# A loaded in two halves, pairs 2 to 6 of W transposed later, pair 2 loaded ahead of the stores of A0, B0 and A0 transposed in the same two banks

## The chip, the cores and the metric

The kernel runs on one core of a Trainium2 chip. The metric is the device time of one execution in microseconds, lower is better. A core has five engines that run their own instruction streams and meet at semaphores: TensorE (PE in the profile; its weight loads are listed as PEld), VectorE (DVE), ScalarE (ACT), GpSimd (POOL) and SyncE (SP). Here nearly all DMA transfers are issued by SP, so SP's stream is the order in which data are asked for.

## The reference

The input `x` has 8 batch entries of 512 tokens and 2048 columns. Two layers are added to it, one after the other:

```python
# layer 0: a low-rank adapter of the batch entry, rank 16
Bx = einsum('bni,bri->bnr', x, B0[adapter_ids])
x = x + einsum('bnr,bor->bno', Bx, A0[adapter_ids])
# layer 1: a dense product, and a gated mixture of 8 adapters of rank 16
base = einsum('btd,od->bto', x, W)                       # W is 2048 x 2048
logits = einsum('btd,ed->bte', x, Wr) + 5 * one_hot(language_ids)
gates = softmax over the two largest logits, zero elsewhere
lora = einsum('bter,bte,eor->bto', einsum('btd,erd->bter', x, A), gates, Bm)
x = x + base + 2 * lora
```

## The kernel before

**Arithmetic.** All large products are float32 made of two parts: an operand is split into a rounded high part and the rest (`wh` and `wl`, `xh0` and `xl0`), and three products (high by high, low by high, high by low) are summed in PSUM. ScalarE makes the high parts, VectorE the low ones. From batch entry 1 on, the dense product goes by a scheme with seven products of halves. It needs sums and differences of blocks of the transposed W; these are computed once, during batch entry 0, and stored to the DRAM tensor `t_scr`.

**The start** (`pe_start`, `act_start`, `dve_start`, `sp_start`). TensorE warms up with 18 transposes of the identity (`warm`), transposes A (`a_transpose`, four groups of 4 blocks), the small weights (`small_transpose`) and batch entry 0 of x (`x_transpose`, 16 units u). For each unit `aux_products` multiplies x by A, Wr and B0 of its entry. Between these steps s = 0 to 15 stand the transposes of all B0 rows (`b0_transpose`, 4 groups) and of all A0 rows (`a0_transpose`, 8 groups). `a0_rows_hi` and `a0_rows_lo` make the two parts of A0; when they are done (semaphore `c_ar` at 2), SP copies 16 rows of them to `a0g` (`G_ROWS`), which TensorE needs for `delta`, and stores all of them to `a_scr` for later entries. `g_products` prepare how layer 1's small products see layer 0. `delta` and `adapt` add layer 0 to x, two units of 128 columns at a time, and `first_hi` and `first_lo` split the result.

**Batch entry 0** (`pe_main`, `act_main`, `dve_main`, `sp_main`). There are 36 slots i, four groups of nine. A slot of the first eight of a group multiplies x by one pair of blocks of W: a first half (`first_products(e, i, 0)`) and a second half of 12 matmuls each. The ninth is the gated adapter product. W comes in as it lies in memory and is transposed here: pair g is loaded by `first_load(g)` into one of two buffers of `raw` (four DMAs of 128 KB), transposed in two halves by `w_transpose(g, h)`, which go through PSUM bank 7 one after the other, and kept by ScalarE (`w_keep(g, h)`) in one of two other buffers of `raw`. From there ScalarE and VectorE split it (`pair_hi`, `pair_lo`), VectorE computes four sums (`w_sums`) into the single buffer `tst`, and SP stores the blocks (`w_store`) and the sums (`w_sums_store`) to `t_scr`.

**What is ordered by what.** Every engine goes through its list in order, and the lists are written out by hand. `first_load(g)` waits until pair g - 2 is transposed; `w_transpose` of a half waits until the half before it is kept; `w_keep(g, 0)` waits for the sums of pair g - 2 and for the landing of the store of pair g - 2 (`d_bs`); `w_sums(g)` waits for the landing of the store of the sums before it (`d_ts`), since there is one `tst`. In SP's list `first_load(i + 5)` stands behind `w_sums_store(i + 2)`. In slot 3 VectorE also makes a difference for the adapter weights (`bt_difference`), whose inputs `bt` come from a load of Bm (`bn`), eight copies on GpSimd and four transposes on TensorE (`bt_transpose`, slots 1 and 2); `bt_store` and `bt_difference_store` write them, and `first_load(8)` reads them back.

In the texts "slot 3" is the part of TensorE's list for i = 3, and (7, 0) is `w_transpose(7, 0)`. A slot without waits lasts about 7 us: two halves of 12 matmuls and some four short transposes or deltas.

## Time and profile before

| | us |
|---|---|
| median of 3 runs | 1611.52 (1611.37 to 1612.34) |
| the profiled execution, whole time | 1611.55 |
| its span, first to last instruction | 1609.8 |
| TensorE busy in it | 1580.3 |
| VectorE busy in it | 1180.3 |
| ScalarE busy in it | 754.5 |

The profiled execution is 0.03 us from the median of the runs. 1.75 us lie outside the span. Times of rows are counted from the start of the span. A row of the timeline gives the start, the duration, the engine, the line of the kernel and the instruction; in brackets stands how long the engine had been idle before it and what released it. Of SP, whose rows say SPq, the duration is that of issuing, not that of the transfer.

### The profile page before, as it was taken

What the parts mean: (1) busy time and instruction counts of PE and PEld (TensorE: products, weight loads), DVE (VectorE), ACT (ScalarE), POOL (GpSimd) and SP (SyncE); (2) the same over time, 40 slices, a digit from 0 to 9 for tenths busy, and PEclk for the clock granted to TensorE, in tenths of its full rate; (3) what the DMA queues carried; (4) which work ended last, traced back from release to release, by engine and by line L of the source; (5) the groups of instructions that cost most, each with busy time, mean ns of one, the idle gap of its engine ahead of it and who ended that gap; (6) DMA issues with size and microseconds to landing.
All of it is one profiled execution on the core that took longest, in us unless ns stands there. A gap on an engine that the chain in (4) does not pass through costs nothing.

```text
span 1609.8 us, 21189 instructions
## 1 busy us (share of the span) xinstructions
PE 1580.3 (98%) x7762; PEld 1334.6 (83%) x7762; DVE 1180.3 (73%) x1603; ACT 754.5 (47%) x988; POOL 9.3 (1%) x19
## 2 busy tenths in 40 slices
PE   8799999999999999999999999999999999999998
PEld 8677887788888888888888888888888888888887
DVE  5664443687678876987778976888769877787665
ACT  6544443254444544454544544445444544445443
POOL 1100000000000000000000000000000000000000
PEclk9899999999999999999999999999999999999999
DMA  9888796879787887779876897879977787576664
GB/s 266 230 232 250 200 251 190 212 213 229 201 224 227 222 212 205 234 212 238 207 217 219 215 233 186 239 230 222 217 197 236 221 226 202 198 231 204 207 222 158
DMA packets 397018, 351.45 MB, mean 218 GB/s; under 512 B 250538, under 2 KB 323546, under 8 KB 395866
## 3 DMA queue, kind: packets, MB, share of 16 engines
q1 hardware_dynamic: 396642, 349.56, 78.7%
q8 instruction: 62, 1.02, 0.3%
q10 hardware_dynamic: 272, 0.52, 0.1%
q14 instruction: 42, 0.34, 0.1%
HBM read 280.75 MB, written 68.82 MB: 217 GB/s over the span
## 4 chain that ended last, share of the span: by engine, by line
PE 92%; issue 3%; DMA 2%; SPq 1%; DVE 1%; POOL 0%; ACT 0%; POOLq 0%; ACTq 0%; DVEq 0%
PE pb L779 27%; PE pb L780 27%; PE pb L781 27%; PE pb L388 4%; PE pb L390 3%; PE pb L542 2%; PE pb L682 1%; DMA t_scr<-tst 1%; DMA a0n<-in_L_cond_A_dram 1%; PE pb L321 0%; DMA bt_scr<-bt 0%; SPq L658 0%; DMA raw<-in_L_cond_W_dram 0%; PE pb L957 0%; POOL xst L1262 0%
## 5 line engine op out<-in xcount | busy, mean ns | idle before, releaser
L775 DVE TENSOR_TENSOR wl<-raw,wh 128x1024 fp32r<-128x1024 f32 (+1 forms) x456 | 554.8, 1217 | 333.9 <-ACT wh L771 333.6
L771 ACT CAST wh<-raw 128x1024 fp32r<-128x1024 f32 (+1 forms) x456 | 477.1, 1046 | 681.6 <-PE pb L781 674.5
L779 PE MATMUL pb<-wh,sh 128*128 128x512 f32 x1568 | 612.9, 391 | 0.5 <-DVE ost L815 0.5
L780 PE MATMUL pb<-wl,sh 128*128 128x512 f32 x1568 | 611.6, 390 | 0.0
L781 PE MATMUL pb<-wh,sl 128*128 128x512 f32 x1568 | 611.2, 390 | 0.0
L781 PEld LDWEIGHTS pb<-wh,sl 128*128 128x128 f32 x1568 | 294.3, 188 | 62.8
L779 PEld LDWEIGHTS pb<-wh,sh 128*128 128x128 f32 x1568 | 294.6, 188 | 56.1 <-DVE wl L775 0.9
L780 PEld LDWEIGHTS pb<-wl,sh 128*128 128x128 f32 x1568 | 294.6, 188 | 55.0
L388 PE MATMUL pb<-awb,xah 128*128 128x304 f32 x512 | 138.7, 304 | 0.0
L390 PE MATMUL pb<-awb,xal 128*128 128x256 f32 x512 | 134.5, 280 | 0.0
L779 PE MATMUL pb<-wh,xh 128*128 128x512 f32 x256 | 105.2, 411 | 0.9 <-DVE ost L815 0.8
L781 PE MATMUL pb<-wh,xl 128*128 128x512 f32 x256 | 101.2, 395 | 0.0
L780 PE MATMUL pb<-wl,xh 128*128 128x512 f32 x256 | 101.1, 395 | 0.0
L388 PEld LDWEIGHTS pb<-awb,xah 128*128 128x128 f32 x512 | 96.4, 188 | 4.4
L390 PEld LDWEIGHTS pb<-awb,xal 128*128 128x128 f32 x512 | 96.5, 188 | 4.2
L621 DVE TENSOR_TENSOR sl<-pool_a,sh 128x512 fp32r<-128x512 f32 x120 | 82.0, 684 | 0.0
L693 ACT COPY raw<-pb 128x512 f32<-128x512 f32 x64 | 37.7, 589 | 77.8 <-PE pb L682 69.1
L616 ACT CAST sh<-pool_a 128x512 fp32r<-128x512 f32 x120 | 73.5, 613 | 0.0
L363 DVE TENSOR_TENSOR xal<-pool_a,xah 128x512 fp32r<-128x512 f32 x88 | 61.3, 696 | 6.0 <-ACT xah L358 5.7
L549 DVE TENSOR_TENSOR pool_a<-pool_a,pb 128x512 f32<-128x512 f32 x88 | 58.6, 679 | 9.1 <-PE pb L542 9.1
L358 ACT CAST xah<-pool_a 128x512 fp32r<-128x512 f32 x88 | 54.8, 623 | 14.5 <-DVE pool_a L267 13.9
L781 PEld LDWEIGHTS pb<-wh,xl 128*128 128x128 f32 x256 | 48.5, 189 | 10.7
(139 smaller groups left out, 1271.3 us busy)
## 6 DMA issues: line engine op xcount, KB each, us to landing
raw<-t_scr SPq DMA_DIRECT2D x392, 512.0 KB, 4.3
xst<-in_x_dram SPq DMA_DIRECT2D x768, 32.0 KB, 3.9
raw<-in_L_cond_W_dram SPq DMA_DIRECT2D x128, 128.0 KB, 3.9
t_scr<-tst SPq DMA_DIRECT2D x32, 512.0 KB, 4.8
raw<-bt_scr SPq DMA_DIRECT2D x28, 512.0 KB, 3.8
out_dram<-ost SPq DMA_DIRECT2D x28, 512.0 KB, 4.5
out_dram<-u SPq DMA_DIRECT2D x28, 512.0 KB, 3.4
t_scr<-raw SPq DMA_DIRECT2D x32, 256.0 KB, 4.0
```

What stands on the lines that cost most here:

```text
L358: e.copy(x_high(n, u).rearrange("p k t -> p (k t)"), two(n, q, kp)).then_inc(c_xh, 1)
L363: e.tensor_tensor(out=x_low(n, u).rearrange("p k t -> p (k t)"), in0=two(n, q, kp), in1=x_high(n, u).rearrange("p k t -> p (k t)").bitcast ...
L388: e.matmul(pb[:, aux_bank(n, u // 8) + t, 0:2 * AW], x_high(n, u)[:, k, toks], cols[:, 0:2 * AW], start=u % 8 == 0 and k == 0, stop=False)
L390: last = e.matmul(pb[:, aux_bank(n, u // 8) + t, 0:LOW], x_low(n, u)[:, k, toks], cols[:, 0:LOW], start=False, stop=u % 8 == 7 and k == 1)
L549: e.tensor_tensor(out=two(n, q, kp), in0=two(n, q, kp), in1=pb[:, delta_bank(n, u), :], op=ALU.add)\
L616: e.copy(sh[:, h % SR, :, :].rearrange("p k t -> p (k t)"), two(b, SUM_QUARTER[product], kp)).then_inc(c_sph, 1)
L621: e.tensor_tensor(out=sl[:, h % SR, :, :].rearrange("p k t -> p (k t)"), in0=two(b, SUM_QUARTER[product], kp), in1=sh[:, h % SR, :, :].rea ...
L771: e.copy(pair_split(wh, g), pair_source(g)).then_inc(c_wh, 1)
L775: e.tensor_tensor(out=pair_split(wl, g), in0=pair_source(g), in1=pair_split(wh, g).bitcast(f32), op=ALU.subtract).then_inc(c_wl, 1)
L779: e.matmul(o, h, wh[:, g % RING, k, :], start=start, stop=False)
L780: e.matmul(o, h, wl[:, g % RING, k, :], start=False, stop=False)
L781: return e.matmul(o, l, wh[:, g % RING, k, :], start=False, stop=stop)
```

## The change

- **A.** The one load of A (1024 KB) is two loads of half its columns, each with a semaphore of its own; the second stands behind the load of x block 1. Groups 2 and 3 of its transposes, and their splits, move from ahead of the first `aux_products` to steps 0 and 1. Four more warm-up transposes stand behind the transposes of x units 0 and 1.
- **B0 and A0.** The transposes of B0 move from steps 3 to 6 to steps 5 to 8, those of A0 rows (first four groups) from 7 to 10 to steps 8 to 11; both now use banks 2 and 3. The second accumulator of `aux_products` moves to banks 0 and 1. `a0_rows_hi` and `a0_rows_lo` move from steps 11 and 12 to 12 and 13. SP issues the load of x block 4 among the loads of B0.
- **End of the start.** (2, 0) leaves it, (1, 1) goes behind the deltas 2 and 3, and the groups of `g_products` around `bx_transpose` and the deltas 0 and 1 are cut one tile earlier. VectorE makes `w_sums(0)` before `pair_lo(0)`.
- **SP.** `first_load(2)` and the load of Bm go ahead of the stores to `a_scr`, which are taken apart.
- **Slots 0 to 3.** The table `W_AT` gives the W transposes of each slot: ahead of the first half, between the halves, behind the second. `pair_hi`, `pair_lo`, `w_sums`, `w_sums_store` of pairs 2 to 5 move by one slot (`next_pair`), and those of pair 5 stand with those of pair 4 in slot 3. The loads of pairs 4 to 8 move one slot later in SP's list. From slot 4 on all is as before.

```diff
@@ pe_main, act_main, dve_main, sp_main @@
+        W_AT = {0: ((), ((2, 0),), ((2, 1),)), 1: (((3, 0),), ((3, 1),), ()),
+                2: (((4, 0),), ((4, 1),), ((5, 0),)), 3: (((5, 1),), ((6, 0),), ((6, 1),))}
+        for i in range(4, SLOTS0):
+            more = i + 3 < SLOTS0 and (i + 3) % 9 != 8
+            W_AT[i] = (((i + 3, 0),), ((i + 3, 1),), ()) if more else ((), (), ())
+        def next_pair(i):
+            return i + 1 if i < 4 else i + 2
...
@@ pe_start @@
-            warm(e)
+            warm(e, 18)
             for u in range(2):
                 x_transpose(e, 0, u)
+            warm(e, 4)
...
-            g_products(e, range(12, 16))
-            w_transpose(e, 1, 1)
+            g_products(e, range(11, 16))
             for u in range(2, 4):
                 delta(e, 0, u)
-            w_transpose(e, 2, 0)
+            w_transpose(e, 1, 1)
@@ dve_main @@
-                pair_lo(e, i + 2)
+                if i:
+                    pair_lo(e, next_pair(i))
...
-                if i + 2 < SLOTS0 and (i + 2) % 9 != 8:
-                    w_sums(e, i + 2)
+                if i and next_pair(i) < SLOTS0 and next_pair(i) % 9 != 8:
+                    w_sums(e, next_pair(i))
                 if i == 3:
+                    pair_lo(e, 5)
+                    w_sums(e, 5)
                     bt_difference(e)
@@ sp_main @@
-                if i + 2 < SLOTS0 and (i + 2) % 9 != 8:
-                    w_sums_store(e, i + 2)
+                if i and next_pair(i) < SLOTS0 and next_pair(i) % 9 != 8:
+                    w_sums_store(e, next_pair(i))
+                if i < 5:
+                    first_load(e, i + 4)
+                if 4 <= i < SLOTS0 - 5:
+                    first_load(e, i + 5)
                 if i == 3:
+                    w_store(e, 5)
+                    w_sums_store(e, 5)
                     bt_store(e)
                     bt_difference_store(e)
-                if i + 5 < SLOTS0:
-                    first_load(e, i + 5)
```

The change moves instructions, and three places show it. The first is SP behind the last row parts of A0 (`c_ar`). Before, the 16 rows for `a0g` are followed by the two stores to `a_scr`, then come the loads of pair 2 (`raw<-in_L_cond_W_dram`):

```order
L1293 DMA a0g<-a0n 16x2048 [waits c_pool,c_ar]
L1293 DMA a0g<-a0n 16x2048
L1293 DMA a0g<-a0p 16x2048
L1295 DMA a_scr<-a0n 128x2048
L1295 DMA a_scr<-a0p 128x2048
L658 DMA raw<-in_L_cond_W_dram 128x2x128 [waits c_wt]
L658 DMA raw<-in_L_cond_W_dram 128x2x128 x3
```

Now pair 2 comes first, then the stores of pair 0, the load of Bm (`ost<-in_L_cond_B_dram`) and one of the two stores; the next load is that of pair 3:

```order
L1308 DMA a0g<-a0p 16x2048
L657 DMA raw<-in_L_cond_W_dram 128x2x128 [waits c_wt]
L657 DMA raw<-in_L_cond_W_dram 128x2x128 x3
L715 DMA t_scr<-raw 128x2x256 [waits c_wc]
L716 DMA t_scr<-raw 128x256
L721 DMA t_scr<-tst 128x4x256 [waits c_t]
L1312 DMA ost<-in_L_cond_B_dram 128x8x256
L1313 DMA a_scr<-a0n 128x2048
L657 DMA raw<-in_L_cond_W_dram 128x2x128 [waits c_wt]
```

What moved: 1 MB of stores each way around the loads of pairs 2 and 3, and the load of Bm, which before stood behind the loads of pair 3.

The second place is the end of TensorE's start. Before, from the last `g_products` to the first matmul of slot 0:

```order
L1066 MATMUL pb<-awb,a0l 128x304
L682 MATMUL pb<-ident,raw 128x128 [waits c_wc]
L682 MATMUL pb<-ident,raw 128x128 x3
L542 MATMUL pb<-bxt,a0g 128x256 [waits c_x1]
L542 MATMUL pb<-bxt,a0g 128x256
L542 MATMUL pb<-bxt,a0g 128x256 [waits c_x1]
L542 MATMUL pb<-bxt,a0g 128x256
L682 MATMUL pb<-ident,raw 128x128 [waits c_wc,d_raw0]
L682 MATMUL pb<-ident,raw 128x128 x3
L682 MATMUL pb<-ident,raw 128x128 [waits c_wc]
L682 MATMUL pb<-ident,raw 128x128 x3
L779 MATMUL pb<-wh,xh 128x512 [waits c_l0,c_wl]
```

Now:

```order
L1077 MATMUL pb<-awb,a0l 128x304
L541 MATMUL pb<-bxt,a0g 128x256 [waits c_x1]
L541 MATMUL pb<-bxt,a0g 128x256
L541 MATMUL pb<-bxt,a0g 128x256 [waits c_x1]
L541 MATMUL pb<-bxt,a0g 128x256
L681 MATMUL pb<-ident,raw 128x128 [waits c_wc]
L681 MATMUL pb<-ident,raw 128x128 x3
L778 MATMUL pb<-wh,xh 128x512 [waits c_l0,c_wl]
```

What moved: the two transposes of pair 2, of which the first waits for its load (`d_raw0`), are no longer ahead of slot 0's products.

The third place is VectorE in slot 3. Before, behind the two `adapt` (`pool_a<-pool_a,pb`) and the two `first_lo` (`xl<-pool_a,xh`) of deltas 10 and 11, come the four sums of pair 5 and the difference `late<-bt`:

```order
L549 TENSOR_TENSOR pool_a<-pool_a,pb 128x512 [waits c_dl] x2
L569 TENSOR_TENSOR xl<-pool_a,xh 128x2x256 [waits c_h0] x2
L702 TENSOR_TENSOR tst<-raw 128x256 [waits d_ts,c_wc]
L703 TENSOR_TENSOR tst<-raw 128x256
L705 TENSOR_TENSOR tst<-tst,raw 128x256 [waits c_t]
L707 TENSOR_TENSOR tst<-raw,tst 128x256 [waits c_t]
L1106 TENSOR_TENSOR late<-bt 128x1024 [waits d_ag,d_gs,c_btc]
```

Now the sums of pair 4, then pair 5's low part, its sums and the difference:

```order
L701 TENSOR_TENSOR tst<-raw 128x256 [waits d_ts,c_wc]
L702 TENSOR_TENSOR tst<-raw 128x256
L704 TENSOR_TENSOR tst<-tst,raw 128x256 [waits c_t]
L706 TENSOR_TENSOR tst<-raw,tst 128x256 [waits c_t]
L774 TENSOR_TENSOR wl<-raw,wh 128x1024 [waits c_wh]
L701 TENSOR_TENSOR tst<-raw 128x256 [waits d_ts,c_wc]
L702 TENSOR_TENSOR tst<-raw 128x256
L704 TENSOR_TENSOR tst<-tst,raw 128x256 [waits c_t]
L706 TENSOR_TENSOR tst<-raw,tst 128x256 [waits c_t]
L1117 TENSOR_TENSOR late<-bt 128x1024 [waits d_ag,d_gs,c_btc]
```

What moved: the sums of pair 4 came into this slot beside those of pair 5, and a wait for the store of the one (`d_ts`) stands ahead of the other.

## Rows read from the trace of the kernel before

**Rows 1.** The page, part 1: busy time, share, instructions.

```profile
PE 1580.3 (98%) x7762; PEld 1334.6 (83%) x7762; DVE 1180.3 (73%) x1603; ACT 754.5 (47%) x988; POOL 9.3 (1%) x19
```

**Rows 2.** Windows: stretch, its length, busy by engine, granted clock, DMA share, GB/s.

```profile
10.00:11.00 1.00, 0.83 (x9) 0.59 (x7) 0.43 (x1) 1.00 (x2) 0.00 (x0) 0.74 1.03 385
...
54.00:55.00 1.00, 0.00 (x0) 0.00 (x0) 0.91 (x3) 0.85 (x2) 0.00 (x0) 0.93 0.90 246
...
65.00:66.00 1.00, 1.00 (x6) 0.75 (x4) 0.00 (x0) 0.00 (x0) 0.00 (x0) 0.95 1.15 348
...
400.00:800.00 400.00, 400.00 (x1926) 337.41 (x1925) 316.81 (x402) 192.28 (x243) 0.00 (x0) 1.00 0.82 219
```

**Rows 3.** Timeline of TensorE in the start: start, duration, instruction, idle before.

```profile
5.51 1.81 PE L321 MATMUL pb<-ident,xst 128*128 128x128 f32 x8
9.25 1.10 PE L963 MATMUL pb<-ident,an 128*128 128x128 f32 x8 [1.94 <-DMA an<-in_L_cond_A_dram]
...
16.68 0.60 PE L388 MATMUL pb<-awb,xah 128*128 128x304 f32 x1
...
50.21 0.63 PE L542 MATMUL pb<-bxt,a0g 128*128 128x256 f32 x4
```

**Rows 4.** Timeline of TensorE around slots 0 and 1.

```profile
57.22 1.11 PE L682 MATMUL pb<-ident,raw 128*128 128x128 f32 x4 [4.34 <-DMA raw<-in_L_cond_W_dram]
60.70 1.12 PE L682 MATMUL pb<-ident,raw 128*128 128x128 f32 x4 [2.36 <-ACT raw L693]
61.47 0.78 PE L779 MATMUL pb<-wh,xh 128*128 128x512 f32 x1
...
71.56 0.65 PE L1094 MATMUL pb<-ident,xst 128*128 128x128 f32 x4 [1.74 <-POOL xst L1262]
```

**Rows 5.** Timeline of TensorE: (6, 0), (7, 0) and (9, 0).

```profile
88.11 0.60 PE L682 MATMUL pb<-ident,raw 128*128 128x128 f32 x4
...
95.39 0.62 PE L682 MATMUL pb<-ident,raw 128*128 128x128 f32 x4
...
111.18 0.66 PE L682 MATMUL pb<-ident,raw 128*128 128x128 f32 x4 [2.26 <-DMA raw<-in_L_cond_W_dram]
```

**Rows 6.** Timeline of SP's queue: start, time of issuing, transfer, count.

```profile
3.94 1.40 SPq L283 DMA_DIRECT2D ost<-in_x_dram  x2
...
43.17 1.25 SPq L1293 DMA_DIRECT2D a0g<-a0n  x2
...
47.71 5.99 SPq L658 DMA_DIRECT2D raw<-in_L_cond_W_dram  x4
...
59.41 0.49 SPq L1301 DMA_DIRECT2D ost<-in_L_cond_B_dram  x1
...
89.43 2.64 SPq L658 DMA_DIRECT2D raw<-in_L_cond_W_dram  x4
...
95.92 0.36 SPq L722 DMA_DIRECT2D t_scr<-tst  x1
...
104.29 2.82 SPq L658 DMA_DIRECT2D raw<-in_L_cond_W_dram  x4
```

**Rows 7.** DMA issues from 0 to 140 us: count, KB each, median us to landing.

```profile
ost<-in_x_dram SPq DMA_DIRECT2D x4, 512.0 KB, 9.1
...
ost<-in_L_cond_B_dram SPq DMA_DIRECT2D x1, 1024.0 KB, 8.0
...
a0g<-a0p SPq DMA_DIRECT2D x1, 128.0 KB, 5.1
```

**Rows 8.** Line 722 (five stores of the sums), 60 to 100 us.

```profile
DMA to landing us min/median/max: 3.8/4.6/6.3
```

**Rows 9.** Timeline of VectorE: sums of pair 5, then sums of pair 6.

```profile
94.33 0.42 DVE L702 TENSOR_TENSOR tst<-raw 128x256 f32<-128x256 f32 x1
...
102.12 0.42 DVE L702 TENSOR_TENSOR tst<-raw 128x256 f32<-128x256 f32 x1
```

**Rows 10.** Timeline of GpSimd: the eight copies of Bm.

```profile
67.41 4.10 POOL L1262 COPY xst<-ost 128x256 f32<-128x256 f32 x8 [37.10 <-DMA ost<-in_L_cond_B_dram]
```

More of the change, by code:

```diff
@@ L1165, in act_start @@
             small_hi(e)
-            for m in range(2, 4):
-                a_hi(e, m)
             x_keep_act(e, 2)
@@ L1208, in dve_start @@
             small_lo(e)
-            for m in range(2, 4):
-                a_lo(e, m)
             x_keep_dve(e, 3)
@@ L1409, in act_main @@
                         sum_hi(e, 1, 0, kp)
-                if i and more:
-                    w_keep(e, i + 3, 1)
+                for n in (1, 2):
+                    for g, h in W_AT[i][n]:
+                        w_keep(e, g, h)
                 if i in (17, 25):
```

132 lines of the change are left out of this document (67 added, 65 removed).

## The prediction

> **What bounds the kernel now.** I read the page first, then TensorE's timeline with its idle times, then SP's and VectorE's lists at the places where TensorE waits. TensorE is busy for 1580.3 us of the span of 1609.8 us [rows 1], and from 400 to 800 us it is never idle [rows 2]; nothing that the change touches lies there. So the change can only move how early TensorE gets through the start and slots 0 to 8, and every microsecond by which it is early at their end is a microsecond of the total. The reader is to look for three things. In the start, TensorE waits 1.94 us for A and its clock then falls: at 10 to 11 us the granted clock is 0.74 on the mean [rows 3, 2], the fall from the level of 2.4 GHz to that of 1.2 GHz. Ahead of slot 0 it waits 4.34 us for pair 2 and 2.36 us for pair 2's first half to be kept [rows 4], and the clock falls again from about 54.9 us (0.93 in the row of 54 to 55) to 65.05 us (0.95 in the row of 65 to 66) [rows 2]. Then come 1.74 us for GpSimd's copies of Bm [rows 4] and 2.26 us for pair 9 [rows 5]. The sum is worked against the profiled execution (1611.55 us with 1.75 us outside the span), which stands 0.03 us from the median, so I take the two as equal.
>
> **The start, to the first aux product.** The half of A asked for first has 512 KB less ahead of it than A as a whole, which held TensorE until 9.25 us; the x transposes end at 7.32 us [rows 3]. I take it as landed by then: the wait of 1.94 us goes, the four added warm-up transposes (about 0.55 us, half of the 1.10 us of eight [rows 3]) lie in what was idle. What comes next late is x block 2, needed two transposes later: it is the first of two loads at 3.94 us and takes about 9 us [rows 6, 7], so 12.9 us, as many bytes being ahead of it as before. The first aux product then starts at about 13.4 us instead of 16.68 us [rows 3], 3.3 us earlier. The two groups of A that move behind it cost their 0.9 us there, so 2.4 us are left; the idle time ahead of x block 2 may let the clock fall once more, which would cost up to 1.7 us (half of 3.4 us, a third of the spell from 54.9 to 65.05 us [rows 2]; bounds of this term 0.7 and 3.4 us). B0's transposes wait less for their loads, A0's stand behind GpSimd's reordering as before; x block 6 is needed about 1 us early, which I count inside the bounds. Take 2.2 us.
>
> **Rows of A0 and the first deltas.** `c_ar` came at 43.17 us [rows 6]. The row splits are one step (1.9 us) later in the lists, which takes back most of the 2.2: SP starts on the `a0g` rows at about 43.3 us. Its last piece is issued about 1.3 us after and takes 5.1 us [rows 6, 7], so 49.6 us at most, 48.6 us with a DMA queue that has no stores of `a_scr` behind. TensorE would be ready for delta 0 at 47.7 us (50.21 less 2.2 less one tile), so here a new wait of 1 to 2 us stands; delta 0 runs at 49.3 us against 50.21 us [rows 3].
>
> **Slot 0.** Behind delta 0 VectorE needs 3.2 us for two `adapt` and two `first_lo`, so slot 0's first product runs at 52.5 us (52.0 to 53.5). Before it ran at 61.47 us [rows 4]: 9.0 us earlier, the waits of 4.34 and 2.36 us and two transposes at the low clock. Pair 2, loaded right behind the rows of `a0g`, is issued from 45.2 us instead of 47.71 us, without the 2 MB of stores ahead that stretched its issue to 5.99 us [rows 6]; it lands at about 51 us and (2, 0) in the middle of slot 0, at 55.7 us, doesn't wait. Its cover is 4.7 us. Slot 0 now has the work that slot 3 had: two halves, two deltas and two W transposes. From (6, 0) to (7, 0) these took 7.28 us with 0.4 us of another product among them [rows 5], so 6.9 us: to 59.4 us.
>
> **Slot 1.** The load of Bm took 8.0 us from 59.41 us [rows 6, 7]; now it is issued at about 49.5 us, lands at 57.3 us, and GpSimd's eight copies take 4.1 us more [rows 10], so 61.2 us against 71.56 us before [rows 4]. TensorE waits 1.7 us, as before. With 7.8 us of work (slot 3's and two more transposes of 0.44 us) slot 2 begins at 69.0 us. Pair 3 has until 61.7 us, and lands by about 60, as 3.9 MB are asked for from 45 us on at some 0.3 MB per us.
>
> **Slot 2.** Pair 4's load has moved behind the second store of `a_scr` and the late rows of `a0g` in SP's list. By the issue times of before for these it is asked for at about 64.6 us, and takes 5.9 us (pair 7's took from 89.43 us to (7, 0) at 95.39 us at most [rows 5, 6]): 70.5 us, a new wait of about 1.1 us at (4, 0). Deltas 8 and 9 end at 74.7 us, VectorE's sums of pair 3 behind them at 78.8 us, and (5, 0) can be kept only then, so slot 3, which now starts with (5, 1), starts at 79.5 us. Before, slot 3 started at 88.11 us [rows 5]. The lead is at its largest about here: 8.6 us, bounds 6.5 and 10.5 us.
>
> **Slot 3 to (9, 0): where the lead goes.** This is the largest term. I count from the start of slot 3. VectorE finishes the sums that stand behind deltas 10 and 11 at +7.8 us. Before these were pair 5's (begun at 94.33 us, stored at 95.92 us, with slot 3's start at 88.11 us [rows 9, 6, 5]), now pair 4's. Three things hang on it. SP stores the sums, and only then loads pair 7: asked for at +8.2, landed at +14.1 us. TensorE has done slot 3 at +9.2 us (it waits some 1.8 us for pair 6, too, whose load has slid in the same way), so (7, 0) waits about 4.4 us; before, (7, 0) ran at +7.3 us with no wait [rows 5]. Second, VectorE must see pair 4's sums landed before pair 5's: 4.6 us (3.8 to 6.3) [rows 8], so pair 5's sums end at +14.0 us. Third, behind them in VectorE's list are the difference (1.2), pair 6's low part (1.2), the gate's first steps (2.1), `adapt` and `first_lo` of delta 12 (2.0), and then pair 6's sums (1.6): +22.0 us. Before, pair 6's sums began at 102.12 us, +14.0 us [rows 9, 5], and ended at +15.6 us. Behind these sums SP stores them, reads `bt` back (0.8) and asks for pair 9, at +23.2 us; from there it took 6.9 us before (104.29 us to 111.18 us [rows 5, 6]), and 5.9 us with an emptier queue. So (9, 0) runs at +29.6 us, with bounds +28.0 and +31.3 us; TensorE's own work with the wait for pair 7 would have it there at +27.8 us. Before it was +23.1 us. The change gives back 6.5 us of 8.6 us: 2.1 us are left.
>
> **Behind (9, 0)** the lists are the old ones and their waits depend on the same chain of sums, so they shift with it. The long wait for pair 7 lets the clock fall, as the wait of 4.34 us did [rows 2, 4]; most of that is hidden, since TensorE is 1.8 us ahead of pair 9. I charge 0.5 us. Sum: 1611.5 - 2.1 + 0.5 = 1609.9 us.
>
> **A rule of the skill.** The landing rows bear the largest term: 512 KB of sums took 3.8 to 6.3 us [rows 8]. The Trainium skill, DMA: Bandwidth & Descriptors, section "Anatomy of one DMA", gives a fixed 2.0 us and bytes over 436 GB/s for a transfer, an estimate of 3.2 us for 512 KB; it was fitted on GpSimd's path, and the rows here lie 0.6 us and more above it. By it the chain of slot 3 would be some 3 us shorter, which is the first rival taken a little further.
>
> **The rivals.** *First, transfers land at their shortest.* In the changed kernel TensorE waits more in slots 2 to 4, and the queue is emptier. With 3.8 us instead of 4.6 us for the store and 5.2 us for pairs 7 and 9 the chain ends at +28.0 us, and at slot 3 Bm and pair 4 would bring another 1 us: 1611.5 - (9.6 - 4.9) = 1606.8 us. For it speaks the DMA share below 0.82 in mid kernel [rows 2]; against it the 0.90 to 1.15 of the rows up to 66 us [rows 2].
>
> *Second, the lead is kept.* If the sums of pair 4 were not what pair 7's load waits for, say because SP and VectorE run well ahead, 8 us would stay: 1603.5 us. Against it stands the order of both lists; only a mistake of mine in reading them makes this one true.
>
> *Third, slower: the clock.* The wait at (7, 0) and the one at (9, 0) each put the clock to the low level. The spell of before lasted 10.2 us [rows 2], and the products ran at half speed from 61.47 us [rows 4] to its end. If the low level lasts 7 us in slot 4 it costs 3.5 us, of which 1.8 us are hidden, and again 3.5 us behind (9, 0) with nothing to hide it: 1609.4 + 1.7 + 3.5 = 1614.6 us. It decides from the point at which TensorE's waits at (7, 0) and (9, 0) are as long as the 1.94 us that preceded the fall at 10.5 us; against it, 2.26 us at (9, 0) let nothing fall before (the last row of a low clock is that of 65 to 66 us [rows 2]).
>
> *Fourth, the start gains nothing*, since the DMA engines are the limit there (1.03 at 10 to 11 us [rows 2]) and the first product of slot 0 comes at 54 us: the lead at slot 3 is 7 us, and 1611.5 us come out.
>
> **How the numbers follow.** My forecast has a chance of 0.52, the first rival 0.18, the second 0.07, the third 0.13, the fourth 0.10. A measurement of this kernel tells about 0.2% (3.2 us) from no change. Faster by over that are the first two rivals and a small tail of the forecast, 0.28; within it are the rest of the forecast and the fourth, 0.59; slower is 0.13. The range runs from 1606.0 us, just past the first rival, to 1615.0 us, just past the third, and leaves out the second and some of the tails, about 0.15. The likeliest case alone has 1608.0 to 1612.0 us, from the bounds of its terms.
>
> **What the profile of the changed kernel would show.** Right: no wait for A, the first aux product near 13.4 us; a wait for `a0g` ahead of delta 0; slot 0 at 52.5 us; GpSimd's copies ending at about 61 us; (5, 1) near 79.5 us; waits of several us at (7, 0) on pair 7's load, VectorE's sums of pair 5 waiting for the store; (9, 0) near 109 us, and from 130 us on a trace shifted by 1 to 2 us. Wrong: slot 0 later than 54 us would say that the start is bound by transfers; (7, 0) less than 10 us behind the start of slot 3 would say that the chain of sums is not the bound, and then the time is below 1606 us; a granted clock at the low level between 100 and 120 us speaks for the third rival.

## The result, and the profile after

The changed kernel takes 1617.07 us (median of 6, 1616.35 to 1618.58); the kernel before, run beside it, 1611.44 us (1610.20 to 1612.34). The ratio is 1.0037, 95% interval 1.0026 to 1.0048: slower by 5.6 us, where 1609.9 us was forecast and the range ended at 1615.0 us. The profiled execution took 1617.13 us with a span of 1615.3 us, 5.5 us more than the span of before.

The page, part 1, answers [rows 1]: TensorE is busy for 1.9 us more and idle for 3.6 us more.

```profile
PE 1582.2 (98%) x7766; PEld 1335.2 (83%) x7766; DVE 1179.7 (73%) x1603; ACT 755.1 (47%) x988; POOL 8.9 (1%) x19
```

Windows, with the columns of [rows 2] (the eighth figure, ahead of the last two, is the granted clock):

```profile
10.00:11.00 1.00, 0.95 (x8) 0.72 (x7) 1.00 (x3) 0.89 (x2) 0.00 (x0) 1.00 1.05 395
...
66.00:69.00 3.00, 3.00 (x12) 2.54 (x11) 0.99 (x1) 1.63 (x2) 0.00 (x0) 0.51 1.06 338
...
100.00:103.00 3.00, 3.00 (x10) 2.51 (x11) 3.00 (x5) 0.59 (x1) 0.00 (x0) 0.50 0.77 240
117.00:123.00 6.00, 5.46 (x15) 4.50 (x16) 2.10 (x7) 1.10 (x2) 0.00 (x0) 0.50 1.10 244
```

The start keeps its clock now (1.00 at 10 to 11 us, 0.74 before), and so does slot 0. In exchange the clock is at 0.50, the level of 1.2 GHz, in three stretches behind it, in slot 1 and behind (7, 0) and (9, 0). Before had none at these times; its own stretch from 54.9 to 65.05 us is gone. The middle of the kernel is as it was: from 400 to 800 us TensorE is busy for all of the 400 us at a granted clock of 1.00.

TensorE in the start, against [rows 3] (in brackets the idle time before and its end):

```profile
12.08 0.66 PE L322 MATMUL pb<-ident,ost 128*128 128x128 f32 x4 [1.13 <-DMA ost<-in_x_dram]
12.50 0.38 PE L387 MATMUL pb<-awb,xah 128*128 128x304 f32 x1
...
38.12 0.63 PE L1042 MATMUL pb<-ident,a0t 128*128 128x128 f32 x4 [1.20 <-ACT a0t L1047]
...
51.46 0.71 PE L541 MATMUL pb<-bxt,a0g 128*128 128x256 f32 x4 [1.30 <-DMA a0g<-a0p]
...
54.78 0.47 PE L778 MATMUL pb<-wh,xh 128*128 128x512 f32 x1 [0.32 <-DVE xl L568]
```

TensorE in slots 0 to 3, against [rows 4, 5]: (2, 1), Bm, (4, 0), and (5, 1), with which slot 3 starts:

```profile
63.38 0.66 PE L681 MATMUL pb<-ident,raw 128*128 128x128 f32 x4 [1.92 <-ACT raw L692]
65.29 0.93 PE L1105 MATMUL pb<-ident,xst 128*128 128x128 f32 x4 [1.26 <-POOL xst L1273]
...
77.13 0.66 PE L681 MATMUL pb<-ident,raw 128*128 128x128 f32 x4 [1.79 <-DMA raw<-in_L_cond_W_dram]
...
86.10 0.66 PE L681 MATMUL pb<-ident,raw 128*128 128x128 f32 x4 [1.01 <-ACT raw L692]
```

Then (6, 0), (7, 0) and (9, 0), against [rows 5]:

```profile
91.02 0.66 PE L681 MATMUL pb<-ident,raw 128*128 128x128 f32 x4 [1.06 <-DMA raw<-in_L_cond_W_dram]
...
99.82 1.11 PE L681 MATMUL pb<-ident,raw 128*128 128x128 f32 x4 [4.15 <-DMA raw<-in_L_cond_W_dram]
...
117.54 1.12 PE L681 MATMUL pb<-ident,raw 128*128 128x128 f32 x4 [2.83 <-DMA raw<-in_L_cond_W_dram]
```

The lead over before is 4.2 us at the first aux product (12.50 against 16.68), 6.7 us at slot 0's first product (54.78 against 61.47), 2.0 us at the start of slot 3 (86.10 against 88.11), and at (9, 0) TensorE is 6.4 us late (117.54 against 111.18). Four transposes take 1.11 or 1.12 us instead of 0.66 behind the last two waits: the clock is low there.

SP's queue, against [rows 6]: `a0g` rows, pair 2, Bm, pair 4, the sums of pair 4, pair 7, pair 9:

```profile
45.21 1.24 SPq L1308 DMA_DIRECT2D a0g<-a0n  x2
...
47.13 3.67 SPq L657 DMA_DIRECT2D raw<-in_L_cond_W_dram  x4
...
52.41 0.53 SPq L1312 DMA_DIRECT2D ost<-in_L_cond_B_dram  x1
...
68.79 6.16 SPq L657 DMA_DIRECT2D raw<-in_L_cond_W_dram  x4
...
93.93 0.36 SPq L721 DMA_DIRECT2D t_scr<-tst  x1
94.33 2.64 SPq L657 DMA_DIRECT2D raw<-in_L_cond_W_dram  x4
...
110.54 2.02 SPq L657 DMA_DIRECT2D raw<-in_L_cond_W_dram  x4
```

ScalarE ahead of (2, 1), and GpSimd's copies of Bm (against [rows 10]):

```profile
61.62 1.21 ACT L563 CAST xh<-pool_a 128x512 fp32r<-128x512 f32 x2 [3.36 <-DVE pool_a L548]
62.74 0.58 ACT L692 COPY raw<-pb 128x512 f32<-128x512 f32 x1
```

```profile
61.52 3.71 POOL L1273 COPY xst<-ost 128x256 f32<-128x256 f32 x8 [32.35 <-DMA ost<-in_L_cond_B_dram]
```

VectorE's first sum of pairs 4, 5 and 6, against [rows 9]:

```profile
92.35 0.42 DVE L701 TENSOR_TENSOR tst<-raw 128x256 f32<-128x256 f32 x1
...
98.48 0.43 DVE L701 TENSOR_TENSOR tst<-raw 128x256 f32<-128x256 f32 x1 [3.45 <-DMA t_scr<-tst]
...
107.00 0.42 DVE L701 TENSOR_TENSOR tst<-raw 128x256 f32<-128x256 f32 x1
```

### The profile page after: what moved, and what is told of

The parts are those of the page before. It is cut to its first block, busy times and chain, and to the rows that moved or that the text cites. A ratio compares the mean times of both kernels' runs of the same rounds, so it can differ in the third digit from the quotient of the medians.

```text
span 1615.3 us, 21197 instructions
## 1 busy us (share of the span) xinstructions
PE 1582.2 (98%) x7766; PEld 1335.2 (83%) x7766; DVE 1179.7 (73%) x1603; ACT 755.1 (47%) x988; POOL 8.9 (1%) x19
## 4 chain that ended last, share of the span: by engine, by line
PE 92%; issue 3%; SPq 2%; DMA 1%; DVE 1%; ACT 0%; POOL 0%; POOLq 0%; ACTq 0%; DVEq 0%
PE pb L778 27%; PE pb L779 27%; PE pb L780 27%; PE pb L387 4%; PE pb L389 3%; PE pb L541 2%; PE pb L681 1%; DMA raw<-in_L_cond_W_dram 1%; SPq L657 1%; DMA a0n<-in_L_cond_A_dram 0%; PE pb L322 0%; PE pb L967 0%; PE pb L497 0%; POOL xst L1273 0%; ACT wh L770 0%
```

## The experiments

All times are medians; "before" ran on the same chip in each group (1611.87 us beside e1 to e4, 1611.53 beside e5 to e8, 1610.95 beside e9 to e12, 1611.63 beside e13 to e15). Ratios are to it, with 95% intervals. The changed kernel was timed in a group of its own, beside 1611.44 us; the medians of before differ by 0.9 us between the groups, so a difference to the changed kernel that is as small can't be told. A trace is one execution, and equal lists don't give equal times: in the eleven traces with the new start, the wait of A0's transposes for `a0t` ends between 36.73 us (e8) and 38.74 us (e4), in the changed kernel at 38.12 us. So a difference of up to 1.4 us to the changed kernel at a slot can come from the start alone. The theory I started from: the lead of the start and of slot 0 is mostly lost ahead of slot 3, and the rest and more in the chain of sums, stores and loads behind it. The rival: one part of the change (the start, SP's order, the table of W) is slow by itself.

### The parts one by one

**e1**, the changed start on the old lists:

```diff
 (before)  up to g_products(e, range(8)): pe_start, act_start, dve_start, sp_start and their helpers as changed
 (kept)    for s, t in enumerate((arh, arl)): e.dma_start(a_scr[s, :, 0:D], t)   # ahead of first_load(e, 2)
```

> Only the front of the change: A in two halves, B0 and A0 transposed in banks 2 and 3 at their new steps, row splits of A0 one step later; the end of the start, SP's order behind the rows of a0g and all slots are those of the kernel before. Theory (the front's lead is eaten by its own waits, and the rows of A0 are ready 2 us later, at 45.2 instead of 43.2 us, as in the changed kernel): the first aux product near 12.4 us, the first delta at 50.5 to 51.5 us, pair 2 landing about 2 us later than before, and 1612 to 1614 us. Rival (the front is worth what it gains at the first aux product, about 3 us, and the loss lies elsewhere): about 1608.5 us.

1613.65 us, ratio 1.0015 (1.0005 to 1.0025). The first aux product comes early here too, and yet `a0g` is asked for at 43.86 us against 43.17, the wait for pair 2 at (2, 0) is 6.21 us instead of 4.34, and (9, 0) is 1.3 us late. The new start alone loses about 2 us. Its execution began early (`a0t` at 36.76 us, 1.4 us ahead of the changed kernel), so the rows came at 43.86 us and not at the 45.2 us expected.

**e2**, the new lists of slots 0 to 3 with the start and the `a_scr` order of before (the cut shows SP's list against that of the changed kernel):

```diff
+            for s, t in enumerate((arh, arl)):
+                e.dma_start(a_scr[s, :, 0:D], t).then_inc(d_as, 16)
             first_load(e, 2)
...
```

> Only the late table: pairs 2 to 6 of W transposed, split, summed and loaded later, with the end of the start that goes with it; front and SP's order around the stores of a_scr are those of before. Theory (the late table alone gives back what it gains, since the load of pair 7 waits for the sums of pair 4 in slot 3 and pair 9's load for those of pair 6): slot 0 near 54 us, 7 us earlier than before, but about 31 us from (5, 1) to (9, 0) instead of 23 us from slot 3's start, (9, 0) at 116 to 118 us and 1616 to 1618 us. Rival (the loss is the front's): 1611 us or less.

1623.15 us, 1.0063 (1.0046 to 1.0080, 4 runs), more than I gave it. Slot 0 starts at 53.80 us, but (2, 1) waits 3.36 us, Bm's transposes 4.78 us, and slot 3 starts at 90.95 us, later than in either kernel. From there to (9, 0) it takes 30.3 us. e11 below is this kernel with SP's new order and nothing else, and takes 7.7 us less. So SP's new order is what makes the new table bearable, and the chain behind slot 3 stays near 30 us, whatever came ahead.

**e3**, SP's new order alone:

```diff
-            for s, t in enumerate((arh, arl)):
-                e.dma_start(a_scr[s, :, 0:D], t).then_inc(d_as, 16)
             first_load(e, 2)
             w_store(e, 0)
             w_sums_store(e, 0)
+            e.dma_start(bn, Bm.rearrange("e (p j) r -> p e j r", p=P)).then_inc(d_bn, 16)
+            e.dma_start(a_scr[0, :, 0:D], arh).then_inc(d_as, 16)
...
             w_sums_store(e, 1)
+            e.dma_start(a_scr[1, :, 0:D], arl).then_inc(d_as, 16)
```

> Only SP's order: pair 2 loaded ahead of the stores to a_scr, the load of Bm ahead of them too, one store behind the sums of pair 1; all else as before. Theory (the stores ahead of pair 2 cost TensorE its 4.3 us wait, and no other part of the change is needed to remove it): pair 2 landed by about 53.5 us, slot 0 at 56 to 57 us, GpSimd's copies ended by 65 to 66 us, and 1607 to 1609.5 us. Rival (what is gained is given back at the next load, since the same bytes are only moved behind): 1611 to 1612 us.

1611.90 us, 1.0001 (0.9991 to 1.0010): nothing, the rival's result. TensorE's timeline (of the fastest execution, 1610.30 us): pair 2 is there, (2, 0) waits 0.50 us instead of 4.34, and the waits for pairs 3 and 5 take the gain back; (6, 0), with which slot 3 starts, stands at 88.00 us against 88.11.

```profile
53.25 0.63 PE L682 MATMUL pb<-ident,raw 128*128 128x128 f32 x4 [0.50 <-ACT raw L693]
...
63.56 0.66 PE L682 MATMUL pb<-ident,raw 128*128 128x128 f32 x4 [3.26 <-DMA raw<-in_L_cond_W_dram]
...
79.11 1.12 PE L682 MATMUL pb<-ident,raw 128*128 128x128 f32 x4 [3.06 <-DMA raw<-in_L_cond_W_dram]
```

**e11**, the changed kernel with the old start:

```diff
 (changed) pe_start, act_start, dve_start, sp_start up to g_products(e, range(8)) and their helpers as before
```

> The changed kernel with the start of before up to the first g_products (one load of A, B0 and A0 transposed at their old steps, row splits at 11 and 12); the lists of SP behind c_ar and of slots 0 to 3 are the changed ones. Theory (the new start costs 1 to 2 us by itself, as it did alone, and the new lists of slots 0 to 3 cost the rest): c_ar at about 43.2 us, slot 0 at 53.5 to 54 us, slot 3 at 85 to 86 us, (9, 0) 31 us behind it, time 1615 to 1616.5 us. Rival (the losses are those of one chain and the start's is hidden behind it): the same slot 3 and the same 1617 us within 0.5.

1615.44 us, 1.0027 (1.0017 to 1.0037), as the theory had it: the new start costs some 1.6 us within the change as well, though the intervals of the two overlap. SP issues the `a0g` rows at 43.48 us and slot 0 starts at 53.75 us, as expected; slot 3 starts at 86.72 us, no earlier than in the changed kernel, and (9, 0) stands at 115.84 us, 29.1 us behind it and not 31. Pair 9 was asked for at 111.15 us, 24.4 us behind slot 3's start as in the changed kernel. What was shorter is its load: the last of its four pieces landed 3.1 us after its issue, and 5.4 us in the changed kernel. So this trace doesn't show where the new start's 1.6 us go.

### The places ahead of slot 3

**e9**, the row splits of A0 one step earlier in the changed kernel:

```diff
-                if s in (12, 13):
-                    a0_rows_hi(e, s - 12)
+                if s in (11, 12):
+                    a0_rows_hi(e, s - 11)
...
```

(and `a0_rows_lo` likewise)

> The changed kernel with the row splits of A0 back at steps 11 and 12. Theory (the split's place is what made delta 0 late: c_ar was seen by SP at 45.2 us in the changed kernel, 43.2 before): SP issues the rows for a0g about 1.5 to 1.9 us earlier, delta 0 runs at about 50.2 us with hardly a wait for a0g, slot 0's first product at about 53.6 us instead of 54.78, and slot 3 and (9, 0) come earlier by no more than that, since waits behind it decide them; time 1616 to 1617 us. Rival (the a0g transfer itself is late, since the queue is full there): the issue comes earlier, the wait at delta 0 stays above 1 us, slot 0 stays at 54.5 us or later and the time at 1617 us.

1614.10 us, 1.0017 (1.0008 to 1.0026), 3.0 us better than the changed kernel, more than either expected. SP's queue and TensorE's timeline:

```profile
41.67 1.25 SPq L1309 DMA_DIRECT2D a0g<-a0n  x2
```

```profile
51.94 0.47 PE L778 MATMUL pb<-wh,xh 128*128 128x512 f32 x1 [0.31 <-DVE xl L568]
```

The wait for `a0g` is gone, slot 0 starts 2.8 us earlier. In this execution the start was early for another reason too (the A0 transposes that wait for `a0t` stood at 37.11 us against 38.12). In e14 below, with the same edit, they stood at 38.03 us and slot 0 started at 52.86 us: 1.9 us from the splits, one step of the lists. At slot 3 (84.42 us) 1.7 of the 2.8 us are left, 1.0 of which the early start may have brought.

**e8**, (2, 0) kept ahead of the `first_hi` of slot 0:

```diff
+                if i == 0:
+                    w_keep(e, 2, 0)
                 for u in DELTAS0.get(i, ()):
                     first_hi(e, u)
```

> The changed kernel with one edit in ScalarE's list of slot 0: (2, 0) is kept ahead of the splits of x units 4 and 5, which wait for VectorE. Theory: TensorE's wait of 1.92 us at (2, 1) goes, but the next thing in TensorE's list, the transposes of Bm, waits for GpSimd's copies until 65.2 us all the same, so slot 1 begins within 0.5 us of before; what may be gained is the low clock from 65.6 to 69.0 us. 1615.5 to 1617.5 us. Rival (this order in ScalarE's list is one of the causes of the loss): 1613.5 to 1615 us.

1618.21 us, 1.0043 (1.0026 to 1.0059, 4 runs), no gain, as the theory had it, though 0.7 us above its range. The trace is of the fastest execution (1615.69 us), whose slot 0 started 1.4 us early, at 53.36 us. The wait of 1.92 us at (2, 1) is gone and stands behind it, up to the same 65.28 us:

```profile
65.28 1.12 PE L1105 MATMUL pb<-ident,xst 128*128 128x128 f32 x4 [4.80 <-POOL xst L1273]
```

**e10**, pair 4 asked for ahead of the late rows of `a0g`:

```diff
             e.dma_start(a_scr[1, :, 0:D], arl).then_inc(d_as, 16)
+            first_load(e, 4)
             e.wait_ge(c_gh, 2)
...
-                if i < 5:
+                if 0 < i < 5:
                     first_load(e, i + 4)
```

> The changed kernel with the load of pair 4 ahead of the wait for the late rows of a0g in SP's list. Theory (pair 4 comes late at (4, 0) because of its place in the list, not because of the bytes): it is asked for at about 64 us instead of 68.8, the wait of 1.79 us at (4, 0) goes, slot 3 starts at about 84.5 us instead of 86.10, and (9, 0) keeps its distance of about 31 us from it, so 116 us instead of 117.5, and the time is 1615 to 1616 us. Rival (the bytes of the stores ahead of it are what it waits for): it is issued earlier but takes the longer to issue and land, (4, 0) waits 1 us or more, slot 3 stays within 0.5 us of 86.1 and the time at 1617 us.

1617.84 us, 1.0039 (1.0026 to 1.0053). Neither expectation holds as it was put: the wait at (4, 0) does go, as the theory said, but slot 3 gains nothing (85.39 us, 0.7 us early, as slot 0 was in this execution at 54.13 us), since pair 5 is the next to be late. (9, 0) comes at 117.94 us. SP issues pair 4 at 63.88 us instead of 68.79, pair 5 at 76.82 us:

```profile
63.88 3.16 SPq L657 DMA_DIRECT2D raw<-in_L_cond_W_dram  x4
...
76.82 3.98 SPq L657 DMA_DIRECT2D raw<-in_L_cond_W_dram  x4
```

```profile
83.57 0.66 PE L681 MATMUL pb<-ident,raw 128*128 128x128 f32 x4 [0.76 <-DMA raw<-in_L_cond_W_dram]
85.39 0.74 PE L681 MATMUL pb<-ident,raw 128*128 128x128 f32 x4 [1.16 <-ACT raw L692]
```

**e5** and **e6**, the two stores of 1 MB to `a_scr` taken out of the start; `a_scr` is filled from x in slots 10 and 12 instead, so that the first layer of the later entries is computed from other numbers. ScalarE's wait for the two stores ahead of the `first_hi` of delta 8 goes with them, and the adapter rows of entry 1 are read in slot 20 instead of 6. e5 is the changed kernel, e6 the one before:

```diff
-            e.dma_start(a_scr[0, :, 0:D], arh).then_inc(d_as, 16)
-            e.dma_start(a_scr[1, :, 0:D], arl).then_inc(d_as, 16)
...
+                if i in (10, 12):
+                    e.dma_start(a_scr[(i - 10) // 2, :, 0:D], x[0, 0:P, :]).then_inc(d_as, 16)
```

> The changed kernel without the two stores of 1 MB from SBUF to a_scr in the start; a_scr is filled in slots 10 and 12 from x instead, and the adapter rows of entry 1 are read in slot 20, so the adapters of later entries are not the reference's. Theory (from 45 to 77 us the transfer engines are the bound, and each MB there costs TensorE about 3 us): 2 MB less bring GpSimd's copies to end at 62 us or earlier, pair 4 to land by 73 us instead of 77.1, slot 3 at 80 to 82.5 us instead of 86.1, and 1611.5 to 1613.5 us. Rival (the order in SP's list and the chain of sums are the bound there too): slot 3 at 85 us or later and 1616 to 1617.5 us.

> The kernel before without the two stores of 1 MB to a_scr, filled later from x as in the other run, so the adapters of later entries are not the reference's. Theory (transfer engines are the bound): pair 2 lands by 51 us instead of 57.2, slot 0 at 54 to 56 us, (9, 0) at 105 to 108 us, 1605 to 1608 us. Rival (given back later, as when the stores were only moved behind pair 2, which brought nothing): 1610 to 1612 us.

e5: 1623.52 us, 1.0070 (1.0053 to 1.0087, 4 runs); e6: 1612.53 us, 1.0006 (0.9996 to 1.0015). The totals say little, as the stores come back later (in e6 TensorE waits 4.5 us for ScalarE's keeps and 5.4 us for loads between 125 and 330 us, in before 0.3 and 3.9 us), so the slots are compared. In e5 slot 3 starts at 86.31 us, as in the changed kernel: with 2 MB less the lead isn't larger, and my theory that bytes hold it falls. Bm's load, asked for at 52.77 us, lands no sooner (62.79 us, 10.0 us later). The wait at (4, 0) is gone, since pair 4 is asked for at 66.03 us; slot 1 has more of the low clock instead (its (3, 1) runs 6.1 us behind (3, 0), against 5.5). In e6 the same 2 MB bring (9, 0) forward by 5.6 us:

```profile
105.57 0.76 PE L681 MATMUL pb<-ident,raw 128*128 128x128 f32 x4 [2.28 <-DMA raw<-in_L_cond_W_dram]
```

So in the kernel before these stores were on the path to (9, 0), and in the changed one they are not on the path to slot 3.

**e13**, e8, e9 and e10 together:

> The changed kernel with the row splits of A0 one step earlier, (2, 0) kept ahead of first_hi in slot 0, and pair 4 loaded ahead of the late rows of a0g: the three places where TensorE was later than forecast ahead of slot 3. Theory (each wait ahead of slot 3 has the next one close behind it, so the three don't add): slot 0's first product at 52 us, no wait at (2, 1), but one of 4 us or more for GpSimd's copies of Bm, then pair 5's load; slot 3 at 83 to 84.5 us, (9, 0) 30 to 31 us behind it, time 1612.5 to 1614.5 us, as with the row splits alone. Rival (the three add): slot 3 at 81 to 82 us and the time at 1611 us or below.

1616.22 us, 1.0035 (1.0021 to 1.0049); with 5 runs from 1613.97 to 1619.50 it can hardly be told from e9, but it is no better. The trace is of the fastest. Slot 0 starts at 52.46 us and slot 3 at 83.46 us, 1.0 us before e9. The three don't add: Bm's copies are late next, and behind them pair 5's load (a wait of 0.51 us at (5, 0)) with its keep.

```profile
63.64 0.72 PE L1105 MATMUL pb<-ident,xst 128*128 128x128 f32 x4 [4.07 <-POOL xst L1274]
...
83.46 0.66 PE L681 MATMUL pb<-ident,raw 128*128 128x128 f32 x4 [1.19 <-ACT raw L692]
```

### The chain behind slot 3

**e4**, each pair's load ahead of the sums' stores in slots 1 to 4, pair 9 ahead of pair 8:

```diff
+                if i < 4:
+                    first_load(e, i + 4)
+                if i == 4:
+                    first_load(e, 9)
+                    first_load(e, 8)
                 if i and next_pair(i) < SLOTS0 and next_pair(i) % 9 != 8:
                     w_sums_store(e, next_pair(i))
-                if i < 5:
-                    first_load(e, i + 4)
...
```

> The changed kernel with one edit in SP's list: in slots 0 to 4 the load of the next pair stands ahead of the store of the sums, and pair 9 is loaded ahead of pair 8. The waits of the loads themselves stay. Theory (the order in SP's list makes pairs 6, 7 and 9 late): the wait of 4.15 us at (7, 0) falls below 1 us, (7, 0) at +9.6 to +10.5 us behind (5, 1) instead of +13.7, the wait of 2.8 us at (9, 0) goes, (9, 0) at +27 to +28 us instead of +31.4, and 1612.5 to 1614.5 us. Rival (VectorE's wait for the store of the sums of pair 4 is the bound, whatever SP does): (9, 0) at +30 us or later and 1616 to 1617 us.

1616.43 us, 1.0025 (1.0015 to 1.0035): the lists moved as the theory had it, the time stayed as the rival had it. The waits for pairs 6, 7 and 9 are gone, (9, 0) stands at 113.33 us (26.1 us behind slot 3's start), and TensorE waits in slot 6 instead, for the low part of x that VectorE makes behind its own wait for the store of the sums. TensorE, then VectorE:

```profile
120.96 0.79 PE L778 MATMUL pb<-wh,xh 128*128 128x512 f32 x1 [3.81 <-DVE xl L568]
```

```profile
115.88 0.43 DVE L701 TENSOR_TENSOR tst<-raw 128x256 f32<-128x256 f32 x1 [3.26 <-DMA t_scr<-tst]
```

**e15**, the sums of pair 5 in a buffer of their own (in `ost`, free between GpSimd's copies and the first outputs):

```diff
+        T5 = (5,)
...
+            buf = tst5 if w in T5 else tst
...
```

> The changed kernel with the sums of pair 5 in a buffer of their own, nothing else. Theory (VectorE's wait of 3.45 us for the store of pair 4's sums is one of the two halves of the slot 3 to (9, 0) chain): (7, 0) waits for its load as before at +13.7 us from slot 3's start, VectorE's sums of pair 5 start about 3.4 us earlier, those of pair 6 too, pair 9 is asked for at about +22 instead of +24.4 us, and (9, 0) runs at about +29.5 us instead of +31.4, since TensorE's own work with the wait for pair 7 ends there; time 1615 to 1616 us. Rival (the load behind the sums is the only half that counts): the same +31 us and 1617 us within 0.5.

1616.37 us, 1.0029 (1.0019 to 1.0040), not to be told from the changed kernel. Pair 5's sums begin at 95.31 us instead of 98.48, but pair 6's at 108.04 us, no earlier: VectorE waits for delta 12, which stands behind TensorE's wait for pair 7. Pair 9 is asked for at 111.57 us, 25.1 us behind slot 3's start (86.47 us), and not at +22. That (9, 0) came at +29.9 us all the same, instead of +31.4, is no success of the theory: pair 9's load took 4.8 us from its first issue to (9, 0) instead of 7.0, a difference that kernels with the same list show too (below).

```profile
100.34 1.12 PE L684 MATMUL pb<-ident,raw 128*128 128x128 f32 x4 [4.30 <-DMA raw<-in_L_cond_W_dram]
...
116.39 0.66 PE L684 MATMUL pb<-ident,raw 128*128 128x128 f32 x4 [0.65 <-DMA raw<-in_L_cond_W_dram]
```

```profile
111.57 2.02 SPq L660 DMA_DIRECT2D raw<-in_L_cond_W_dram  x4
```

**e7**, e4 and e15 together:

> The changed kernel with the loads ahead of the stores of sums in slots 0 to 4 (as in the run with loads first), and pair 5's sums in a buffer of their own (the free half of ost), so that VectorE need not wait for the store of pair 4's sums. Theory (VectorE's wait of 3.5 us in slot 3 is what was left of the 8 us given back): slot 6's products start 3 to 4 us earlier than with loads first alone, at 117 to 118 us instead of 120.96, and 1612 to 1613.5 us. Rival (VectorE's own work in slots 3 to 5 is the bound, two sets of sums and the difference in one slot): less than 1.5 us, 1615 to 1616.5 us.

1612.79 us, 1.0011 (1.0002 to 1.0021), 4.3 us below the changed kernel, while e4 and e15 alone gave 0.6 and 0.7. Against e4 the buffer brings slot 6's first product forward by 3.8 us (120.96 to 117.20). Two waits that start from the same sums cover each other, and only both together make room:

```profile
96.23 0.63 PE L684 MATMUL pb<-ident,raw 128*128 128x128 f32 x4 [0.37 <-ACT raw L695]
...
117.20 0.80 PE L786 MATMUL pb<-wh,xh 128*128 128x512 f32 x1 [3.26 <-DVE xl L571]
```

### Versions meant to be faster

**e14**, e7 with the row splits of e9:

> The changed kernel with the row splits one step earlier, each pair's load ahead of the stores of the sums in slots 1 to 4 (pair 9 ahead of the read of bt), and the sums of pair 5 in a buffer of their own. Theory (the two gains lie at different places, 3.0 us ahead of slot 0 and 4.3 us in slots 3 to 6, and add): slot 3 at 84.4 us, slot 6's first product at about 114.5 us, time 1609 to 1611 us, a little below the kernel before. Rival (the second chain gives the first gain back, as it did with other leads): 1612 to 1613 us.

1611.17 us, 0.9998 (0.9989 to 1.0007), 5.9 us below the changed kernel and level with before, 0.2 us above the theory's range. The two gains (3.0 and 4.3 us) nearly add, as the theory had it, but beat nothing.

**e12**, the kernel before with its loads ahead of the sums' stores and the sums of pairs 3, 5 and 7 in a second buffer:

```diff
+                if i < 3:
+                    first_load(e, i + 5)
+                if i == 4:
+                    first_load(e, 9)
+                    first_load(e, 8)
                 if i + 2 < SLOTS0 and (i + 2) % 9 != 8:
                     w_sums_store(e, i + 2)
...
```

> The kernel before with each pair's load ahead of the store of the sums in SP's list in slots 0 to 4 (pair 9 ahead of the read of bt), and the sums of pairs 3, 5 and 7 in a buffer of their own. Theory (the wait of 2.26 us for pair 9 at (9, 0) is the list's doing): (9, 0) runs without a wait for its load at about 109 us instead of 111.2, VectorE is not late with xl in slot 6 as it was when this was done to the changed kernel (3.3 us), because its sums of pair 6 are not held by a store, and the time is 1608.5 to 1610.5 us, below both kernels. Rival: as in the changed kernel another wait (xl of delta 13 or the keep of a half) takes the place of this one, 1611 to 1612.5 us.

1610.30 us (1608.60 to 1612.49), 0.9995 (0.9986 to 1.0004): no difference that can be told. In the trace, of the fastest execution (1608.60 us), (9, 0) is transposed at 107.67 us without a wait, 3.5 us early, of which 1.1 us were there at slot 3's start already (87.02 us). The next pair gives most of it back: (10, 0) waits 2.87 us and stands at 118.30 us, against 118.88 before.

```profile
118.30 0.66 PE L685 MATMUL pb<-ident,raw 128*128 128x128 f32 x4 [2.87 <-DMA raw<-in_L_cond_W_dram]
```

## Why the prediction was wrong

**The start: the first term right, its fate not.** A's wait is gone and the first aux product came at 12.50 us (13.4 forecast), with no fall of the clock. The wait of 1.13 us for x block 2 ahead of it was in the forecast. But the lead of 4.2 us was used up behind it, inside the start: 0.9 us for the two groups of A as counted, and then waits that the forecast had not, or had only inside its bounds: 0.65 us for B0 (0.39 before, and I had written that it would wait less), 0.60 us for x block 5, 0.74 us for x block 6, and 1.20 us for the copy `a0t`. The last is in all eleven traces with the new start: groups 3 and 4 of A0's transposes now stand in the same step, and the fifth needs ScalarE's copy of the fourth. I wrote that A0's transposes stand "as before" and didn't read that step. By (0, 0) TensorE stood at 40.05 us against 40.27, and with the row splits a step later SP came to the `a0g` rows at 45.21 us, 1.9 us behind the forecast and 2.0 behind before. e9 and e14 show that this step of the lists was worth 1.8 to 1.9 us at slot 0.

**The lead at slot 3 is the step that failed**: 8.6 us forecast (bounds 6.5 and 10.5), 2.0 measured. Slot 0 started at 54.78 us instead of 52.5 (2.3 us, outside its bounds of 52.0 to 53.5). From there to slot 3 I had 27.0 us and it took 31.3: 1.9 us for the wait at (2, 1), which the sum didn't have; about 1.7 us for 3.4 us at the low clock from 65.6 us on; 0.7 us more at (4, 0), of which e10 shows that another wait would have stood there; less 0.4 us at Bm. That makes 3.9 of 4.3 us; the other 0.4 us is spread over the work of three slots. The wait at (2, 1) is one of order: ScalarE keeps (2, 0) behind the two `first_hi` of deltas 4 and 5, which wait for VectorE's `adapt` until 61.6 us. I had used slot 3's distance of 6.9 us for slot 0, though VectorE has more in its list there. e8 shows that this wait was no loss of its own, since Bm's copies ended at 65.2 us (forecast 61.2): Bm's load was issued at 52.41 us (49.5) and took 9.1 us to land (8.0). e13 puts three of the places right and wins 2.6 us of 6.6 at slot 3, about 0.5 of them by an early start (`a0t` at 37.64 us). Each was close behind the other, and a sum of terms that takes one late thing in each slot can't see that.

**The chain behind slot 3 was right, and a little longer.** From the start of slot 3, forecast and measured: sums of pair 4 done +7.8 and +7.8 us, pair 7 asked for +8.2 and +8.2, (7, 0) +14.1 and +13.7, sums of pair 5 done +14.0 and +13.9, pair 9 asked for +23.2 and +24.4, (9, 0) +29.6 and +31.4, the latter just past its bound of 31.3. The give-back is 8.4 us, not 6.5. Pair 9 was asked for 1.2 us later: about 0.5 us because VectorE's sums of pair 6 were done later (it was idle for 0.63 us ahead of delta 12, which stood behind products at the low clock), about 0.7 us because SP took 1.45 us to issue the two reads of `bt` instead of 0.8. And from its first issue to (9, 0) passed 7.0 us instead of 5.9. The last number is no property of the change: in the eight other runs with this order around pair 9 (e2, e5, e8 to e11, e13, e15) it was 4.7 to 6.6 us, and (9, 0) stood at +29.1 to +32.6 us. What sets it was not tried. That the chain gives the lead back is shown by e7, with both of its halves removed (4.3 us); the buffer's half also by e7 against e4 (3.6 us), the loads' half by e7 against e15 (3.6 us). Neither shows in the time when it is removed alone.

**Behind (9, 0) the charge of 0.5 us was the wrong size, and luck covered it.** The low clock stood there from shortly before 117 us to about 123.5 us, and (9, 1) came 6.03 us behind (9, 0), against 3.27 us before: a cost of 2.8 us with nothing to hide it, and a lag of 9.1 us. Before and now:

```profile
114.45 0.60 PE L682 MATMUL pb<-ident,raw 128*128 128x128 f32 x4
...
126.58 0.63 PE L682 MATMUL pb<-ident,raw 128*128 128x128 f32 x4 [1.07 <-DMA raw<-in_L_cond_W_dram]
...
131.74 0.63 PE L682 MATMUL pb<-ident,raw 128*128 128x128 f32 x4 [0.90 <-DVE raw L668]
```

```profile
123.57 0.60 PE L681 MATMUL pb<-ident,raw 128*128 128x128 f32 x4
...
138.22 0.63 PE L681 MATMUL pb<-ident,raw 128*128 128x128 f32 x4 [0.33 <-DVE raw L667]
```

Between these rows the kernel before has several waits that the changed one has not, or has shorter, and 2.6 us come back (the lag is 6.5 us at the last row). Another 1.0 us comes back between 280 and 300 us, where before waits 2.87 and 1.95 us and the changed kernel 2.22 and 1.61 us.

**Which makes the sum:** 6.6 us at slot 3 and 1.9 us in the chain make -8.5 of the +2.1 us forecast at (9, 0), so -6.4; behind it the charge of 0.5 us was 2.8 us for the clock, and 3.6 us came back: 1611.55 + 6.4 + 2.8 - 3.6 = 1617.15 us, against 1617.13 measured. By parts of the change, the ratios of e1 (1.0015) and e11 (1.0027) add up to that of the whole (1.0037) within their intervals: some 2 us are the new start's, some 4 us those of the new table with SP's order.

**The rule on landings.** The six stores of the sums of pairs 1 to 6 in the changed kernel landed like this:

```profile
DMA to landing us min/median/max: 3.8/4.6/8.1
```

and VectorE went on 4.6 us after the issue at 93.93 us. The 3.2 us worked out from the section "Anatomy of one DMA" of the Trainium skill, DMA: Bandwidth & Descriptors, were not reached; the row decided rightly, and no part of the miss hangs on it.

**The rivals.** The first two ended on the wrong side. The fourth had the right sign in what it watched (slot 0 later than 54 us says that the start gives little) but took the rest of my sum with it; and the reason that it gave, transfers, is not the one that the runs show, since the place of the row splits, the one edit of e14 ahead of slot 0, brought it back to 52.86 us. The third, the clock, came nearest (1614.6 us) and its sign was there: the clock was low behind (7, 0) and (9, 0), as after waits of 4.15 and 2.83 us. Its 3.5 us behind (9, 0) were 2.8. But its 7 us in slot 4 were 3.4, hidden as far as pair 9 was late anyway, it had nothing for the 3.6 us that came back, and the loss of 6.6 us ahead of slot 3 was no part of it. My chance of 0.13 for slower was too small because all the rivals kept the lead at slot 3.

**What stays open.** How much of the 6.6 us at slot 3 each place costs by itself: the places cover each other, and e13 still leaves 4.0 us, for which Bm's copies, pair 5's load with its keep and the low clock are the candidates that its timeline shows. Asking for Bm earlier was not tried. Open is also what sets the landing of pair 9's load, which moves (9, 0) by up to 2.3 us between kernels that have the same order there.

## What to carry to other kernels

A lead at the front of hand-ordered queues is worth only what the next late thing leaves of it. So don't carry one lead through several stages: write down for each stage when the second and the third input would be ready too, and read every engine's list at each step that now holds two things that depend on each other. A step of one engine's list that feeds a far chain (here `a0_rows_hi`, 1.8 to 1.9 us) can cost as much as the visible wait that is removed (1.94 us for A); and where two waits start from one event, take both away or neither.
